# A selective-scan and attention kernel whose first stage is put in another order

## What is computed

```
mod = c @ w + b;  shift, scale, gate = split(mod, 3)          # layer 0, twice: for the scan and for the MLP
h   = layernorm(x) * (1 + scale) + shift
x   = x + gate * (ssm(h, forward) + flip(ssm(flip(h), backward)))
      # ssm: xs, z = h @ in_w;  xs = silu(xs);  dt, B, C = xs @ xproj_w;  dt = softplus(dt + dt_bias)
      #      state = state * exp(dt * A) + dt * xs * B;  y = state . C + xs * Dskip;  (y * silu(z)) @ out_w
x   = x + gate * (silu(h @ w1) * (h @ w2) @ w3)
ada = silu(cond) @ ada_w.T + ada_b -> gamma1, gamma2, scale1, scale2, shift1, shift2
x   = x + attention(ln(x) * (scale1 + 1) + shift1) * gamma1
x   = x + mlp(ln(x) * (scale2 + 1) + shift2) * gamma2
```

## Time and profile before

| | us |
|---|---|
| median of three runs | 3436.22 |
| the profiled execution's own time | 3437.39 |
| its span | 3435.6 |
| first transpose of x (PE L914) | starts at 51.40 |
| first product with in_w (PE L822) | starts at 54.38 |
| first scan tile (DVE L1356) | starts at 97.62 |
| first weighing (POOL L543) | starts at 100.38 |

### The profile page before, as it was taken

The page is one execution under the profiler, slowest core; times in us unless marked ns, Lnnn a source line. Parts: engine busy times, 40 slices in busy tenths (PEclk is TensorE's granted clock), DMA queues, the critical chain, the costliest instruction groups (busy, mean ns, idle before and its releaser), DMA issues. The chain is left out here.

```text
span 3435.6 us, 60533 instructions
## 1 busy us (share of the span) xinstructions
PE 3272.0 (95%) x23720; PEld 2705.5 (79%) x23720; DVE 2798.0 (81%) x3009; ACT 2803.2 (82%) x4960; POOL 2501.9 (73%) x1104
## 2 busy tenths in 40 slices
PE   7999999999899999999989999999999999999998
PEld 6889898974488988897368898899637898888744
DVE  2899999976299999996639999999554999999761
ACT  1989999964498999995559999999356999999734
POOL 1899999960098999994029999999204999999700
PEclk9999999998999999999999999999989999999989
DMA  3221211100111121220021222212002221111000
GB/s 131 84 64 56 72 56 64 62 32 13 53 62 64 62 69 52 70 68 25 1 70 57 64 70 64 63 58 68 13 1 78 68 64 68 55 57 56 31 13 7
DMA packets 57088, 187.71 MB, mean 55 GB/s; under 512 B 6626, under 2 KB 12770, under 8 KB 55906
## 3 DMA queue, kind: packets, MB, share of 16 engines
q1 hardware_dynamic: 56802, 183.84, 16.0%
HBM read 180.65 MB, written 3.16 MB: 54 GB/s over the span
## 5 line engine op out<-in xcount | busy, mean ns | idle before, releaser
L543 POOL TENSOR_TENSOR states<-states,c_rows 128x1024 f32<-128x1024 f32 x1020 | 2394.7, 2382 | 499.0 <-DMA c_rows<-c_spill 411.8
L1356 DVE TENSOR_TENSOR_SCAN states<-decay,bank 128x512 f32<-128x512 f32 x2048 | 2350.9, 1203 | 214.8 <-ACT decay L684 143.0
L684 ACT ACTIVATE decay<-dt,a_log 128x512 f32<-128x512 f32 x2048 | 1307.2, 712 | 0.5 <-DVE states L1356 0.5
L937 PE MATMUL bank<-ident,states 128*128 128x128 f32 x8192 | 1237.3, 274 | 18.2 <-POOL states L543 0.3
L926 PE MATMUL bank<-ident,inflow_tok 128*128 128x128 f32 x6144 | 1046.3, 279 | 59.8 <-DVE states L1356 42.9
L678 ACT ACTIVATE inflow_tok<-dtx_tok,b_tok 128x512 f32<-128x512 f32 x1536 | 995.4, 714 | 61.8 <-PE bank L927 58.5
L937 PEld LDWEIGHTS bank<-ident,states 128*128 128x128 f32 x8192 | 955.0, 142 | 50.4 <-POOL states L543 47.9
L926 PEld LDWEIGHTS bank<-ident,inflow_tok 128*128 128x128 f32 x6144 | 707.5, 141 | 241.6 <-issue 128.9
L927 PE MATMUL bank<-b_diag,dtx_tok 128*128 128x128 f32 x4096 | 794.5, 276 | 0.0
L927 PEld LDWEIGHTS bank<-b_diag,dtx_tok 128*128 128x128 f32 x4096 | 621.0, 192 | 0.0
L1444 DVE TENSOR_REDUCE decay<-bank 128x1 f32<-128x512 f32 x256 | 159.7, 684 | 68.0 <-PE bank L1118 67.7
(11 more groups left out here) (152 smaller groups left out, 2039.3 us busy)
## 6 DMA issues: line engine op xcount, KB each, us to landing
c_rows<-c_spill SPq DMA_DIRECT2D x256, 512.0 KB, 3.7
xproj_w<-in_xproj_w SPq DMA_DIRECT2D x32, 320.0 KB, 4.3
in_w<-in_in_w SPq DMA_DIRECT2D x16, 512.0 KB, 4.9
in_w<-in_fc_w SPq DMA_DIRECT2D x8, 512.0 KB, 5.3
xproj_w<-in_w SPq DMA_DIRECT2D x8, 512.0 KB, 5.2
xproj_w<-in_fc_w SPq DMA_DIRECT2D x4, 1024.0 KB, 4.8
y_gated<-in_mod_w SPq DMA_DIRECT2D x1, 2048.0 KB, 7.4
x_ahead<-in_x SPq DMA_DIRECT2D x4, 512.0 KB, 5.6
```

Of the source, the lines that this page charges most:

```text
L543: pool.tensor_tensor(pair, pair, c_row, ALU.mult).then_inc(weighed, 1)
L684: act.activation(decay[:, r % SLOTS * KI + k, :], dt[:, d, k, :], ACT.Exp, scale=a_neg[:, d, k, s:s + 1]).then_inc(decay_ready, 1)
L937: last = pe.matmul(banks[KI + t][:, k * P:(k + 1) * P], states[:, r % SLOTS * KI + k, t * P:(t + 1) * P], ident[:], is_transpose=True, sta ...
L1356: dve.tensor_tensor_scan(states[:, slot, time], decay[:, slot, time], banks[k % INFLOW_BANKS][:, time], 0.0, ALU.mult, ALU.add).then_inc(s ...
```

## The change

The loads are issued in another order: cond, x of batch 0, mod_b, set 0 of mod_w, set 1, in_w, set 2, xproj_w, SSM, set 3, gate_w, gate_b (now to 4 partitions only), REST. `first_loaded` is split into five semaphores; sets 1 and 2 share `mod_loaded`. The sets are computed one at a time, each in a bank of its own: 0 and 1 ahead of PE's `look_ahead`, 2 between `look_ahead` and `prepare`, 3 and the gates between `prepare` and the first row. The gates of all four batches come from one product for each pair of gates and half of the contraction: cond (128 x 4) is stationary, 512 columns of gate_w move, and the result lies on 4 partitions. DVE computes set 0 between the variance and the normalising, sets 1 and 2 ahead of `prepare`, set 3 and the gates behind it; negating A and capping scale_mul go to places inside `prepare`. POOL builds `d_diag` behind `look_ahead`. SP waits for the gates only after C is spilled and the second in_w and xproj_w are issued, and waits for their write only ahead of loading x_in (which now holds them).

```diff
-        gate_b = c_rows[:, 0, :, :].rearrange("p a (g d) -> p (a g) d", d=D)
-        gate_all = decay[:].rearrange("p k l -> p (k l)").rearrange("p (b g d) -> p b g d", b=B, g=4)
+        gate_b = c_rows[0:B, 0, :, :].rearrange("p a (g d) -> p (a g) d", d=D)
+        gate_all = x_in[0:B, :, :]
...
@@ sync
-            for name in FIRST:
-                load(sp, name, first_loaded)
+            load(sp, "cond", cond_loaded)
             sp.dma_start(x_ahead[:], x_rows[0]).then_inc(ahead_loaded, 16)
+            def load_mod(i, signal):
+                sp.dma_start(mod_w[:, :, i, :, :], inp["mod_w"][:, :, i, :, :]).then_inc(signal, 16)
+            load(sp, "mod_b", mod_first_loaded)
+            load_mod(0, mod_first_loaded)
...
+            load_mod(1, mod_loaded)
             for kc in range(KD):
                 load_in(0, kc)
+            load_mod(2, mod_loaded)
             for kc in range(KI):
                 load_xproj(0, kc)
             for name in SSM:
                 load(sp, name, ssm_loaded)
+            load_mod(3, mod_last_loaded)
+            load(sp, "gate_w", gates_loaded)
+            sp.dma_start(gate_b, inp["gate_b"].partition_broadcast(B)).then_inc(gates_loaded, 16)
             for name in REST:
                 load(sp, name, rest_loaded)
-            sp.wait_ge(gate_ready, 4 * B)
-            sp.dma_start(gate_spill..., gate_all[0:1, ...]).then_inc(gate_spilled, 16)
-            sp.wait_ge(gate_spilled, 16)
             spill(0)
...
             for kc in range(KI):
                 load_xproj(1, kc)
+            sp.wait_ge(gate_ready, 2)
+            sp.dma_start(gate_spill, gate_all.rearrange("b g d -> b (g d)")).then_inc(gate_spilled, 16)
...
                     if d == 0 and at == 2:
+                        if b == 0:
+                            sp.wait_ge(gate_spilled, 16)
                         sp.dma_start(x_in[:], x_rows[b]).then_inc(x_loaded, 16)
@@ scalar
-            act.wait_ge(first_loaded, 16 * len(FIRST))
+            act.wait_ge(cond_loaded, 16)
             act.activation(silu_cond[:], cond[:], ACT.Silu).then_inc(cond_ready, 1)
...
             for s in range(NS):
+                if s == DT_EXP_AT[0]:
+                    act.wait_ge(ssm_loaded, 16 * len(SSM))
+                    act.activation(a_exp[:], a_log[:], ACT.Exp).then_inc(a_exp_done, 1)
+                    act.wait_ge(cap_ready, 1)
+                    act.wait_ge(sign_ready, 1)
+                    act.activation(qk_scale[:, 0:H], scale_cap[:], ACT.Exp).then_inc(q_scale_ready, 1)
                 prepare(0, 0, s)
@@ tensor
+            def modulate(i):
+                c = cond if i < 2 else silu_cond
+                for w in range(2):
+                    for f in range(KD):
+                        at = (w * KD + f) * B
+                        for kc in range(KD):
+                            last = pe.matmul(banks[KI + i][:, at:at + B], mod_w[:, kc, i, w, f * P:(f + 1) * P], c[:, kc, :],
+                                             start=(kc == 0), stop=(kc == KD - 1))
+                last.then_inc(mod_mm, 1)
+            def gates(h):
+                c = silu_cond if h else cond
+                for kc in range(KD):
+                    last = pe.matmul(banks[KI + h][0:B, :], c[:, kc, :], gate_w[:, kc, 2 * h:2 * h + 2, :]...,
+                                     start=(kc == 0), stop=(kc == KD - 1))
+                last.then_inc(gate_mm, 1)
...
+            pe.wait_ge(mod_first_loaded, 32)
+            modulate(0)
+            pe.wait_ge(mod_loaded, 32)
+            modulate(1)
             for at in range(NS):
                 look_ahead(0, at, None)
+            modulate(2)
             for at in range(NS):
                 prepare(0, 0, at, first=True)
+            pe.wait_ge(mod_last_loaded, 16)
+            modulate(3)
+            pe.wait_ge(gates_loaded, 32)
+            pe.wait_ge(mod_sum, 2)
+            gates(0)
+            gates(1)
@@ vector
             for s in range(NS):
+                if s == AHEAD_POWER_AT:
+                    modulate(0)
                 look_ahead(0, s)
+            modulate(1)
+            modulate(2)
             for s in range(NS):
+                if s == C_COPY_AT + 1:
+                    dve.wait_ge(rest_loaded, 16 * len(REST))
+                    dve.tensor_scalar(scale_cap[:], scale_mul[:], MAX_SCALE_MUL, None, ALU.min).then_inc(cap_ready, 1)
...
+                if s == DT_READY_AT[0]:
+                    dve.wait_ge(a_exp_done, 1)
+                    dve.tensor_scalar(a_neg[:], a_exp[:], -1.0, None, ALU.mult).then_inc(a_ready, 1)
                 prepare(0, 0, s)
+            modulate(3)
+            gates(0)
+            gates(1)
```

More of the change, by code:

```diff
@@ L258, in build @@
         mod_ready = sem("mod_ready")
+        mod_half = sem("mod_half")
         gate_mm = sem("gate_mm")
@@ L354, in build @@
         fc1_ready = sem("fc1_ready")
-        FIRST = ["cond", "mod_w", "mod_b", "gate_w", "gate_b"]
         SSM = ["dt_b", "a_log", "d_skip", "out_w"]
         REST = ["w3", "qkv_w", "row_b", "scale_mul", "proj_w", "fc1_b"]
-        home = dict(cond=cond[:], mod_w=mod_w, mod_b=mod_b[:], gate_w=gate_w, gate_b=gate_b, dt_b=dt_b[:], a_log=a_log[:],
+        home = dict(cond=cond[:], mod_b=mod_b[:], gate_w=gate_w, dt_b=dt_b[:], a_log=a_log[:],
                     d_skip=d_skip[:], out_w=out_w[:], w3=w3[:], qkv_w=qkv_w[:], row_b=row_b[:], scale_mul=scale_mul[:],
                     proj_w=proj_w[:], fc1_b=fc1_b[:])
-        ROW_INPUTS = ("gate_b", "row_b", "scale_mul")
+        ROW_INPUTS = ("row_b", "scale_mul")
         def load(eng, name, signal):
@@ L508, in _ @@
                                pattern=[[-1, P]], channel_multiplier=1).then_inc(ident_ready, 1)
[L509 to L514, removed]
             pool.memset(qk_scale[:, H:2 * H], -1.0).then_inc(sign_ready, 1)
@@ L546, in _ @@
                 look_ahead(0, s)
+            pool.wait_ge(ident_ready, 1)
+            pool.wait_ge(ssm_loaded, 16 * len(SSM))
+            for d in range(2):
+                for k in range(KI):
+                    pool.tensor_scalar(d_diag[:, d, k, :], ident[:], d_skip[:, d, k:k + 1], None,
+                                       ALU.mult).then_inc(diag_ready, 1)
             for s in range(NS):
@@ L592, in _ @@
         def _(act):
-            act.wait_ge(first_loaded, 16 * len(FIRST))
+            act.wait_ge(cond_loaded, 16)
             act.activation(silu_cond[:], cond[:], ACT.Silu).then_inc(cond_ready, 1)
-            act.wait_ge(ssm_loaded, 16 * len(SSM))
-            act.activation(a_exp[:], a_log[:], ACT.Exp).then_inc(a_exp_done, 1)
-            act.wait_ge(cap_ready, 1)
-            act.activation(qk_scale[:, 0:H], scale_cap[:], ACT.Exp).then_inc(q_scale_ready, 1)
+            act.preload_act_table_set("exp_and_others")
             def ln(b, i):
                 n = (b * 3 + i - 1) * TT
+                if b == 0 and i == 1:
+                    act.wait_ge(mod_ready, 4)
                 def shift(t):
@@ L773, in _ @@
             pe.sem_inc(summed, TILE_CREDIT)
-            for i in range(4):
+            def modulate(i):
                 c = cond if i < 2 else silu_cond
@@ L944, in skip_term @@
                     pe.wait_ge(y_ready, b * 2 * TT + t + 1)
+                elif b == 0 and t == 0:
+                    pe.wait_ge(diag_ready, 2 * KI)
+                    pe.wait_ge(mod_sum, 4)
+                    pe.wait_ge(gate_ready, 2)
                 for k in range(KI):
@@ L1024, in batch @@
                 pe.wait_ge(y_low_ready, (b + 1) * KI)
+                pe.wait_ge(ssm_loaded, 16 * len(SSM))
                 project(0, 0)
@@ L1256, in spread, with gates @@
+            def gates(h):
+                if h == 0:
+                    dve.wait_ge(gates_loaded, 32)
+                dve.wait_ge(gate_mm, h + 1)
+                dve.tensor_tensor(gate_all[:, 2 * h:2 * h + 2, :].rearrange("b g d -> b (g d)"), banks[KI + h][0:B, :],
+                                  gate_b[:, 2 * h:2 * h + 2, :].rearrange("b g d -> b (g d)"), ALU.add).then_inc(gate_ready, 1)
             def spread(b, i, t, eps):
```

83 lines of the change are left out of this document (31 added, 52 removed).

## The result

The changed kernel took 3402.91 us (median of four runs, 3398.71 to 3405.88) against 3435.52 (four runs, 3434.76 to 3437.71): a ratio of 0.9903, 95% interval 0.9886 to 0.992, 32.6 us. Measured once more, beside other runs of the kernel before, it was 3402.09 against 3436.73, ratio 0.9905 (0.989 to 0.992). The forecast was 3406.2 and a gain of 30.0. The profiled execution took 3403.86 with a span of 3402.1, 33.5 less than the earlier trace rows.

A forecast was written before the change was run, and what follows sets the result against it. One chain with hardly a gap up to the first scan tile was taken to bound the opening. 33.5 - 1.0 - 2.5 = 30.0 us off gave 3407.4 profiled, 3406.2 on the median's scale; range 3400.5 to 3413.

The forecast's parts named there:

- The mechanism: Opening up to the first scan tile: one chain with hardly a gap; whatever the first scan tile gains, 30.0 us, the end gains.
- The load: Opening loads: x, three sets and in_w, 3.1 MB, have landed so that PE starts set 1 at 12.0 us.
- slow load: Rival, opening loads: 3.1 MB at 220 GB/s ends at 16.3, 4.3 us late; time 3410.5; chance 0.13.
- PE up to in_w: PE from set 1 to in_w: 3.5 us a set, transposes 1.94; in_w starts at 20.9, 33.5 us earlier.
- The clock in in_w: First in_w products: 2.0 us more at half clock than before, which loses 1.0 us.
- early-clock rival: Rival, set 2 and first in_w group run at full clock: 1.7 and 2.0 us come off; 3402.5; chance 0.09.
- Prepare: From in_w to the last transpose of dt*xs: unchanged 39.3 us, moved work fits in gaps; transposes end at 61.2.
- Between prepare and row 0: PE behind prepare: set 3 takes 1.8 us, gates 3.8, only 2.5 is paid; first scan tile at 67.6.
- cold-clock rival: Rival, before row 0: narrow set 3 brings the clock down, set 3 and gates cost 5.4 us more; 3411.6; chance 0.07.
- POOL: First rows: first weighing 4.0 us after the scan, 1.2 more lag, cost 0; rival that it sets the pace 3412.1, chance 0.06.
- The rest: From the first scan tile to the end: rows keep their pace, so no gain or loss is charged there.

## Why the prediction was right, step by step

**The mechanism** was right. The first stage is one chain, and over two profiles of each kernel it became 26.9 to 29.1 us shorter, where the forecast had 30.0; the end gained no less. The old order with the new gates splits it: 10 to 11 from the gates' products and gate_b, 17 to 18 from the order. That kernel is also the plainest sign that the end follows the first scan tile: 10.3 to 10.8 us there, 9.1 in the time. With gains of 25 to 35 us the other kernels follow less closely, by up to 6 us either way, so the rule holds to some us and not better.

**The load** was the term ahead of the first scan tile that was mis-sized most: 12.0 forecast, 14.46 and 13.93 measured for set 1 (13.93 to 15.60 over four kernels). I had taken 3.1 MB at the rate at which mod_w and gate_w had moved. With x, in 1 KB pieces, and set 0 first, 208 to 310 GB/s moved up to 8.75 us instead of 419. The rival "slow load" was half right: late by 2 to 3.6, not 4.3, and the size of the sets' pieces is at most a part of it.

**PE up to in_w**: a set took 3.57 (forecast 3.5), the transposes 1.95 (1.94) and set 2 3.41. in_w started at 22.91 (20.9), as late as the load less 0.4.

**The clock in in_w.** From in_w's first product to the end of prepare's transposes it took 39.7 us in the first profile and 40.1 in the second, before 39.3. Over the five profiles with this order up to here 0.4 to 1.3 were lost, where I charged 1.0: the clock rose 3.9 to 5.7 us behind in_w's first product, before 3.0. The early-clock rival did not come: PE worked without a gap from 14.46, and the records with in_w stayed at half clock until 26.8 (10 of them from 23.0 to 26.8, then 7 in 1.2 us). With wide products ahead, the full clock came for sets 0 and 1 but not for in_w, although PE worked almost without a gap from 1.5 to 19.9 us; it was granted at half from 10.2 to 13.6 and from 17.0 to 23.8. The sentence of the Trainium skill that I weighed there ("TensorE: Matmul & The Clock Gate", Part 1: The HAM clock gate) makes sustained work enough. The trace does not agree, and the measurement decides. What it is in the sets or the transposes that went with the falls is open; the fall at 10.2 came behind set 0 with no transpose before it.

**Prepare**: last transpose ended at 62.60, 61.2 forecast. The moved exp, negation and cap were free, as said: in the profile after, DVE's copy of C, scale_cap and the first dt follow as before.

**Between prepare and row 0**: set 3 took 1.85 (1.8). The gates took 5.3 in the first profile and 3.6 in the second (3.8 forecast). The cold-clock rival came in part: its cost was 1.7 on the gates in one execution and none in the other, not 5.4. The first scan tile came at 70.30 and 68.49, for 67.6.

**POOL**: 4.3 behind the first scan tile (4.0 forecast) and not paid. The kernel that loads the C rows earlier shows it: rows 2, 4 and 8 at the same distance to the hundredth.

**The rest** is the term that was furthest off, and the forecast had put it at nothing: I said that DVE's pace in the rows would stay, and the rest with it. The rows did keep their pace (row 8 of the first batch starts 41.0 behind the first tile, before 41.1), but the rest as a whole was 6.2 us shorter in the profile pair, and it moves by as much from one execution to the next with the granted clock. For the profiled execution the two errors have opposite signs: 2.7 us lost ahead of the first scan tile, 6.2 gained behind it, so 3403.86 came for 3407.4. That the forecast's number was met within 3.5 us is therefore in part luck. Without the 6.2 it would have been missed by 2.7 on the other side, still inside the range. Whether some of the 6.2 comes with the change on the average is open. For it, the changed kernel's two measurements stand for 33 to 35 us where the first stage accounts for 27 to 29. Against it, other kernels with the changed order have rests up to 3337.2, and its three near variants (gates ahead of set 3, 4 KB runs, C rows before the gates) gained 29.4, 31.6 and 24.8.

## What to carry to other kernels

Where a program opens with one chain, put the input and the part of the parameters that it needs first, and look for the load that shares a semaphore with a later one: moving sets 1 and 2 behind prepare took 1 to 3 us more off the first scan tile. Price work on a nearly full engine by what it displaces: PE's 0.9 us at a time put into the rows cost 5.2 in all, 3.0 of it in one small DVE instruction that nobody had priced. Before reading a few microseconds of total time, find an anchor in the trace (here the first scan tile) behind which both programs are alike, and see how far that part moves by itself.

## What the runs showed of the hardware

The rest of this program, some 3332 us of the same work, took 3328.3 to 3338.0 over twelve profiles, about 0.47 us more for each microsecond of half clock (130 to 150 us of it), and the two profiles of the kernel before gave the same 3338.0 and the same 150 us. TensorE's clock in the first stage was granted differently in two executions of the same program (gates 5.3 and 3.6). The wide gates directly behind set 3 began at half clock in five of six profiles, and directly behind prepare's transposes in none of four; the cause was not parted.

Until 8.75 us the loads moved at 208 to 310 GB/s when the first pieces were of 1 and 2 KB, against 419 with pieces of 16 KB and against some 400 later on. With 4 KB instead of 2 KB pieces, 1.02 MB instead of 0.76 moved in the microseconds 5 to 8.

An 8-element DVE instruction took 3.19 us once and 0.17 twice in the same kernel. The slow one ended 0.03 us behind a weighing of POOL that lay wholly inside it. Whether POOL held it was not tried.
